# Front slots of a four-layer kernel in another order: probabilities turned behind the next scores, attention product behind the queries

## The reference, cut to what matters

```python
q, k, v = split(norm(x) @ Wq + bq), split(ctx @ Wk + bk), split(ctx @ Wv + bv)
scores = einsum('bhqd,bhkd->bhqk', q, k) * scale
attn = softmax(scores, axis=-1)
o = einsum('bhqk,bhkd->bhqd', attn, v)
x = x + o.reshape(B, S, 128) @ Wo + bo
```

## Time and profile before

| what | value |
|---|---|
| median of 3 runs | 2417.6 us (2416.79 to 2418.31) |
| profiled execution | 2425.08 us, its span 2423.3 us |
| PE busy | 2342.5 us, 97% of the span |
| DVE busy | 1870.4 us, 77% |
| ACT busy | 1505.6 us, 62% |
| POOL busy | 1216.4 us, 50% |
| mean granted clock of TensorE | 0.987 |
| front slots in the span | from about 1610 us to 1757 us |

### The profile page before, as it was taken

How to read it: one execution, slowest core, us unless ns; L and a number is a source line. 1 busy time by engine, 2 the same in 40 slices (tenths; PEclk the granted TensorE clock), 3 DMA queues, 4 the chain that set the end, 5 groups by cost and what they waited for, 6 DMA issues and landing times.

```text
span 2423.3 us, 61019 instructions
## 1 busy us (share of the span) xinstructions
PE 2342.5 (97%) x25478; PEld 1422.6 (59%) x25478; DVE 1870.4 (77%) x3328; ACT 1505.6 (62%) x2190; POOL 1216.4 (50%) x1028
## 2 busy tenths in 40 slices
PE   8998999999999999999999999987899999999998
PEld 6785566666666666666666666655445555455443
DVE  6989989999999999999999989957756765445222
ACT  3444666666666666666666666654477777566443
POOL 2336777777777777777777777722211121111000
PEclk9999999999999999999999999998899999999999
DMA  3000000000000000000000100002010110120110
GB/s 129 9 7 6 2 2 28 11 8 7 28 11 8 7 28 11 13 2 28 10 13 3 35 2 11 2 4 89 9 38 9 41 33 15 55 86 29 38 41 22
DMA packets 36183, 56.30 MB, mean 23 GB/s; under 512 B 6396, under 2 KB 20868, under 8 KB 35656
## 3 DMA queue, kind: packets, MB, share of 16 engines
q1 hardware_dynamic: 35912, 52.40, 6.8%
HBM read 51.19 MB, written 1.19 MB: 22 GB/s over the span
## 4 chain that ended last, share of the span: by engine, by line
PE 73%; DVE 19%; ACT 4%; issue 3%; POOL 1%; DVEq 0%; ACTq 0%; POOLq 0%
PE w L1621 9%; PE w L1611 9%; PE w L679 6%; PE w L660 6%; PE w L670 5%; DVE turned L1161 4%; PE w L430 4%; PE py L700 4%; PE w L724 3%; PE w L753 3%; PE w L734 2%; DVE norm L1168 2%; PE pt L783 2%; PE py L787 2%; PE w L1750 2%
## 5 line engine op out<-in xcount | busy, mean ns | idle before, releaser
L441 ACT ACTIVATE prob<-logit 128x512 f32<-128x512 f32 x224 | 137.9, 632 | 285.0 <-DVE logit L449 285.0
L1611 PE MATMUL w<-qT,m_fc 128*128 128x512 f32 x544 | 267.8, 605 | 0.4 <-ACT turned L1875 0.4
L1346 POOL TENSOR_TENSOR straight_odd<-straight_odd,turned 128x1024 f32<-128x1024 f32 x96 | 226.6, 2371 | 65.6 <-DVE turned L1161 65.6
L471 POOL TENSOR_TENSOR prob<-prob,rden 128x1024 f32<-128x1024 f32 x112 | 213.9, 1909 | 91.0 <-DVE rden L460 91.0
L1161 DVE TENSOR_TENSOR turned<-w,rot 128x512 f32<-128x512 f32 x384 | 245.5, 681 | 0.0
L1346 POOL TENSOR_TENSOR straight<-straight,turned 128x1024 f32<-128x1024 f32 x96 | 226.7, 2372 | 36.1 <-DVE turned L1161 36.1
L1340 POOL TENSOR_TENSOR straight_odd<-straight_odd,rnorms 128x1024 f32<-128x1024 f32 x96 | 180.7, 1903 | 118.2 <-DVE rnorms L1182 118.2
L1168 DVE TENSOR_REDUCE norm<-sq 128x16 f32<-128x1024 f32 x192 | 224.2, 1209 | 0.0
L490 POOL TENSOR_TENSOR fresh_roots<-fresh_means,eps 128x1 f32<-128x1 f32 x64 | 12.3, 191 | 386.1 <-DVE fresh_means L478 386.1
L1340 POOL TENSOR_TENSOR straight<-straight,rnorms 128x1024 f32<-128x1024 f32 x96 | 180.7, 1903 | 42.9 <-DVE rnorms L1182 42.9
L679 PE MATMUL w<-b_wqkv,m_proj 128*128 128x512 f32 x384 | 190.4, 618 | 1.9 <-DVE logit L449 1.9
(11 more groups left out here) (290 smaller groups left out, 5353.3 us busy)
## 6 DMA issues: line engine op xcount, KB each, us to landing
b_wqkv<-gates SPq DMA_DIRECT2D x64, 256.0 KB, 3.6
b_wqkv<-in_b_wqkv SPq DMA_DIRECT2D x18, 512.0 KB, 3.5
ctxT<-in_ctxT SPq DMA_DIRECT2D x64, 64.0 KB, 1.8
b_wo<-in_b_wo SPq DMA_DIRECT2D x6, 512.0 KB, 4.0
m_fc<-in_m_fc SPq DMA_DIRECT2D x1, 2304.0 KB, 8.5
m_proj<-in_m_proj SPq DMA_DIRECT2D x1, 2304.0 KB, 13.1
m_fc<-in_m_fc SPq DMA_DIRECT2D x8, 256.0 KB, 3.4
m_proj<-in_m_proj SPq DMA_DIRECT2D x8, 256.0 KB, 3.4
```

The source lines that it names most:

```text
L471: pool.tensor_tensor(flat, flat, k.rden[:, s, :, None].broadcast_to([P, HEADS, SEQ]), ALU.mult).then_inc(k.prob_ready, 1)
L1346: pool.tensor_tensor(k.straights[s][:, i, :, :], k.straights[s][:, i, :, :], k.turned[:, i, :, :], ALU.add).then_inc(added, 1)
L1611: pe.matmul(claim(("hidden", J, c)), k.m_fc[:, x, c * P:(c + 1) * P], k.m_xT[:, q, :], start=True, stop=True).then_inc(k.ring_full, 1)
```

## The change

On TensorE the probabilities of a work are no longer transposed at the end of the slot that holds its scores, in two halves around `rows`, but in the next slot, all eight in one go. If this work and the next use the same bank, they are turned ahead of the next scores, else behind them. The attention product goes from behind `keys` to behind `queries`. On ACT the copy of the turned probabilities goes from the slot's end to the next slot, behind `turned_x`, `fresh_normalise` and the layers' part, ahead of `front`; `turned_rows` now goes ahead of `exp`. In the last front slot the probabilities are turned at its end, so that the expert slots find them as before. DVE's, POOL's and SP's lists are the same. No instruction is added or taken away.

```diff
--- before.py
+++ after.py
@@ -1743,16 +1743,13 @@
         pe.wait_ge(d.k8_ready, started(u + 1))
         pe.matmul(k.py[:, P:2 * P], k.s_oT[:, :], k.s_w[:, n, 3, :], start=True, stop=True).then_inc(d.y_psum, 1)
 
-    def turn_pairs(W, pairs):
+    def turn_probs(W):
         w = logits_bank(k, W)
         pe.wait_ge(d.exp, PHANTOM + W + 1)
-        for h in pairs:
+        for h in range(PAIRS):
             mm = pe.transpose(w[:, h * P:(h + 1) * P],
                               k.prob[:, W % 2, 2 * h:2 * h + 2, :].rearrange("p a m -> p (a m)"), k.ident[:, :])
-        return mm
-
-    def turn_probs(W):
-        turn_pairs(W, range(PAIRS)).then_inc(d.pT_psum, 1)
+        mm.then_inc(d.pT_psum, 1)
 
     def occupy():
 
@@ -1764,16 +1761,20 @@
     def front_slot(u, work, before, before2):
         if work:
             turn_x(work[2], u)
+        together = before and before2 and on_w0(before[2]) == on_w0(before2[2])
+        if together:
+            turn_probs(before2[2])
         if before:
             scores(before[2])
         layers_in_slot(u, "scores")
+        if before2 and not together:
+            turn_probs(before2[2])
         if work:
             keys(*work, u)
+            values(work[0], work[2], u)
+            queries(work[0], work[2])
         if before2:
             attend(before2[2], u)
-        if work:
-            values(work[0], work[2], u)
-            queries(work[0], work[2])
         if u in PRODUCT_AT:
             turn_quantised(PRODUCT_AT[u])
         layers_in_slot(u, "end")
@@ -1781,12 +1782,10 @@
             occupy()
         if before2:
             turn_rows(before2[2], u)
-        if before:
-            turn_pairs(before[2], range(PAIRS // 2))
         if before2:
             rows(before2[0], before2[2], u)
-        if before:
-            turn_pairs(before[2], range(PAIRS // 2, PAIRS)).then_inc(d.pT_psum, 1)
+        if before and u == LEAD - 1:
+            turn_probs(before[2])
 
     def turn_quantised(q):
         pe.wait_ge(k.f.quantised, q + 1)
@@ -1946,17 +1945,19 @@
         if job:
             gelu(job, 3)
         layers_in_slot(u, "turned x")
+        if before2 and u < LEAD:
+            turned_probs(before2[2])
         if work:
             front(work[0], work[2])
         layers_in_slot(u, "front")
         if u < LEAD:
             if u in PRODUCT_AT:
                 turned_quantised(PRODUCT_AT[u])
-            if before:
-                exp(before[0], before[2])
             if before2:
                 turned_rows(before2[0], before2[2], u)
             if before:
+                exp(before[0], before[2])
+            if before and u == LEAD - 1:
                 turned_probs(before[2])
         if u in GATES_TURN_AT:
             e, q = GATES_TURN_AT[u]
```

## The result

| | before | after |
|---|---|---|
| median | 2417.19 us (2416.2 to 2418.31, 4 runs) | 2436.49 us (2435.96 to 2436.87, 4 runs) |
| ratio after / before | | 1.0077 (1.0064 to 1.0090) |
| profiled execution, its span | 2425.08, 2423.3 us | 2436.58, 2434.8 us |
| PE busy | 2342.5 us | 2349.6 us |
| mean granted clock | 0.987 | 0.984 |

The changed kernel is slower by 19.3 us. The forecast was 2424.3 with a range of 2414 to 2431: the direction was right, the size was not.

What follows compares the result with a forecast made beforehand. Chains of waits were taken to bound each slot: PE and ACT's at 6.66 us, DVE's almost as long at 6.43. Slot terms summed to +6.7 us on the 2417.6 us median, giving 2424.3 us, range 2414 to 2431.

Steps and rivals of the forecast that it cites:

- slot 13: Half-clock slot with PE as the bound: +0.9 at half clock, -2.0 at full clock; +0.9 taken.
- slot 9: Slot at clock 0.85 that took 7.78 us: 7.47 at full clock, 8.5 at part, +0.3 taken.
- slots 8, 12: After a quantisation, DVE's sum waits less for ACT's copy: 9.62 to 8.27 us, -2.7 for the two.
- slots 2 to 4: First slots: -0.95 for slot 2, +0.6 each for slots 3 and 4; put together at +1.2 us.
- the steady slot: Undisturbed slot (5, 6, 10): late copy and attention product lengthen it from 6.66 to 7.47 us, +0.81 each.
- R': Start of the next slot's `rows` weight load, R being this slot's; forecast R+7.47 undisturbed, R+10.13 where scores wait for the copy.
- a joined slot: Slots 3, 14, 15, both tiles in bank w1: scores wait for the copy; 14 and 15 go 16.39 to 20.26, +3.9.
- rival (b): Slots 14 to 16: clock falls after PE's nearly 3 us wait; +3 to +9 us, 2427 to 2433; chance 0.19.
- the base: Profiled before took 2425.1 us, plain median 2417.6; the forecast difference of +6.7 was put on the median.
- Rival (c): Clock kept where it was lost: slot 13 -2.9, slot 3 -2.4 at full clock; sum +1.4, 2419; chance 0.20.
- the PE-ACT ring: In-slot chain where exp waits for copies behind queries and attention product; removing it is worth at most 0.23 us a slot.
- Rival (a): Attention not late, ACT's copy not held by fresh normalisation, DVE binds at 6.43 us; 2409.5 to 2414.5; chance 0.10.

Runs made afterwards that it cites:

- the second of before: Kernel before, unchanged, profiled again beside its first repeat's plain runs: 2417.75 us, ratio 0.9999; its trace's span is 2415.7 us.
- The kernel with the copy first: Kernel after, with ACT's copy of the turned probabilities put ahead of the fresh normalisation in the front slots: 2421.97 us, ratio 1.0024.
- the kernel with works 0, 1 and 12 to 14 as before: Kernel after, with works 0, 1 and 12 to 14 handled as in before except their attention product, still behind the queries: 2424.27 us, ratio 1.0023.
- The experiment with the attention product alone: Kernel before, with only the attention product moved behind the queries, probabilities still turned in their own slot: 2415.84 us, ratio 0.9996.
- the second trace of after: Kernel after, unchanged, run and profiled once more: two runs of 2434.36 and 2437.48 us, ratio 1.0072, span 2432.6.

## Why the prediction came out as it did

The sum by slots, in us; measured is the first trace of after less the second of before, and its total is the difference of the two spans, 19.1:

| part | predicted | measured |
|---|---|---|
| slots 5, 6, 10 | +2.4 | +2.4 |
| slots 7, 11 | 0 | 0 |
| slot 13 | +0.9 | +0.8 (-2.0 against the first trace) |
| slot 9 | +0.3 | +0.8 |
| slots 8, 12 | -2.7 | -1.2 |
| slots 14, 15 | +3.9 | +10.8 |
| slots 2 to 4 | +1.2 | +3.7, with slots 0 and 1 |
| slots 16, 17 | +0.7 | +0.4 |
| ahead of slot 0 | none | +1.4 |
| sum | +6.7 | +19.1 |

**Right: the steady slot.** Each mark of the working was hit: y_all at R+2.96, the copy behind it without idle time, rden idle on the product, R' at R+7.46 for 7.47. The kernel with the copy first shows the cause by taking it away: 6.79.

**Right: R' of a joined slot at full clock.** 10.13 was worked out, 10.18 measured where PE was kept busy. In that kernel the whole change costs 7.3 us (2424.49 against 2417.18), near the sum's 6.7. The nearness is partly luck: slots 14 and 15 lose 4.7 there for 3.9 (the sum set 20.3 against the 16.39 of the first trace, the other two have 15.62), slots 2 to 4 more than forecast, and slots 16 and 17 gain 2.7 from a clock of 1.00 where before has 0.87 and 0.88.

**Wrong: the clock in the joined slots, rival (b).** The working named a joined slot's 6.1 us of PE work in 10.1 with a wait of nearly 3 us, named the rule by which the clock would fall, and then took the full-clock figure for the sum, R' = R+10.13, with 0.19 for the rival. The evidence for full clock was slots that are busy for 77% of their length, and 6.1 in 10.1 is 60%: no row of before supported full clock at such a share. (The two slots of that row were not alike either: 8.58 us at 0.90 and 7.81 at 1.00.) That is the step that failed: measured were 13.08 and 13.38 us at clocks of 0.59 and 0.50. The rival's price per slot was good (2.8 estimated, 2.90 and 3.20 measured), but half clock also fell on slot 4 (0.71 of the clock, 0.97 in before), which the rival hadn't priced; slots 16 and 17 have as much of it in before. And it is not only a matter of the wait: the kernel with late turning only where banks differ lost the clock after a wait of 1.08 us, and the one with these works as before kept it after the same wait.

**Wrong: the base.** The profiled execution of before was 7.5 us over the median, and the prediction saw this and put the difference on the median unchanged. That is sound only if the excess lies outside the slots that are compared. Of the 7.6 us between the spans of the first two traces, 3.3 lie ahead of R of slot 2 and the rest inside: slot 13 at 9.46 and slot 9 at 7.78 are 6.66 in an execution like the plain ones, slots 14 and 15 are 7.81 each and not 8.2. Slot 9's term was +0.3 for a loss of 0.8 for that reason, and the term of slot 13 came out right by luck, as +0.9 was reasoned for a slot at half clock and +0.79 measured for one at full clock. Rival (c) priced slots 3 and 13 at full clock as a gain of the change: in slot 13 the two later traces of before have it already.

**Half right: slots 8 and 12.** The mechanism came as forecast: DVE's sum waited 1.49 us and now waits 0.20, under the 0.5 that was named.

```profile
1690.39 1.14 DVE L2140 SCALAR_TENSOR_TENSOR x_all<-xs,f_scale,x_all 128x128 f32<-128x128 f32 x4 [0.20 <-ACT xs L1979]
```

Slot 8 came to 8.53 (8.27 forecast), but slot 12 to 9.53: at a clock of 0.70 PE is busy for 8.73 us of it, and PE became the bound. The term had left the clock of these slots out, though before has 0.74 and 0.76 there.

**Mis-sized: slots 2 to 4.** The forecast of -0.95 for slot 2 depends on the execution: from the first turn of x (slot 0) to R of slot 2 the kernel after took 29.21 us in one trace (clock 0.94) and 27.97 in the other (0.99), before 28.84 in its second and third (0.98). At like clocks that is -0.87, near the forecast; the first trace of after lost it to half clock. Slot 4 went to 10.49 at 0.71, for 8.9 forecast at nearly full clock; in the kernel with works 0, 1 and 12 to 14 as before, whose work 2 is late too, slot 4 had full clock and took 8.50. So the order costs about 0.4 there and the clock 2.0, as far as one trace can tell. The 1.4 us ahead of slot 0 lie in code that the change doesn't touch; the second trace of after, which is 3.3 us ahead of the first at slot 2, suggests that they are chance.

**Wrong: why the change should help at all.** The first paragraph said that the edit cuts the PE-ACT ring because the queries come 1.0 us earlier. The experiment with the attention product alone refutes it: `front` waits for that product. The prediction had noted this wait itself, further down, and not carried it back. It did no harm to the number, since the late attention set the slot anyway.

**Rival (a)** needed the copy to start by R+2.3, while the working had the transposes end no earlier than R+2.75; the kernel with the copy first measured R+2.67 and 6.79 us. The rival contradicted the prediction's own figure and deserved no chance in this kernel. Its 6.43 us was nearly the true floor nevertheless: 6.36 was reached by putting the exponential first and turning in one go.

## What to carry to other kernels

Before a copy is moved in an engine's queue, look at what stands ahead of it there and what that waits for: here one place behind an operation that waits for GpSimd cost 0.67 us in every steady slot. When a change puts a wait into a slot, look in the trace for a slot that waits as long, or has as little work in it, and still shows full clock. If there is none, as here for 6.1 us of work in 10.1, put the half clock into the forecast and not among the rivals, and look at the slots behind it as well. Where there are such slots, the runs here say only that it can go either way (1.99 and 1.09 us for the same scores behind the same wait of 1.08 us). And where a profiled execution is longer than the plain runs, find the slots that hold the excess before any term is priced against them.

## What the runs showed of the hardware

- Work that nobody uses can pay: three occupying products in each of three slots (2.74 us of PE in slot 14) took 11.4 us off the kernel (2435.92 to 2424.49).
- One and the same program differs by much of what a change like this costs: plain runs of the kernel before, without any edit, went from 2411.3 to 2423.9 us, 12.6 us against 19.3, and two of its traces differ by 7.6 us at equal work, by half-clock stretches in slots 9 and 13 that one has and the other hasn't and by 3.3 us ahead of R of slot 2, while slot 16 is at full clock in the slower one (11.49 us) and at 0.87 in the other (13.17). What starts such a stretch isn't known.
- The clock fell behind a wait of 1.08 us in one kernel (late only where the banks differ) and not behind the same wait in the next (works 0, 1 and 12 to 14 as before), with PE busy for 73% of the ten microseconds ahead of the scores in both. What decides stays open.
